# A two-layer decoder on one core: in the state space, four of sixteen input products per group made token-major by ScalarE and turned back by TensorE

## The reference, cut to what matters

```
xn = layernorm(x); x_in, z = split(xn @ W_in)            # 256 inner channels
u  = silu(causal_conv4(x_in) + b)
dt_r, B, C = split(u @ W_xproj)                          # 8, 16 and 16 columns
dt = softplus(dt_r @ W_dt + b_dt)
for n in 16 states:  h[n,t] = h[n,t-1]*exp(dt[t]*A[n]) + dt[t]*u[t]*B[t,n]
y  = sum_n h[n,t]*C[t,n] + u*D;  out = x + (y*silu(z)) @ W_out
```

## Time and profile before

| | us |
|---|---|
| median of 3 runs | 1837.51 (1835.39 to 1838.07) |
| the profiled execution, its own time | 1837.73 |
| its span in the profile | 1836.0 |
| PE busy | 1472.0 (80%) |
| DVE busy | 1420.9 (77%) |
| POOL busy | 895.3 (49%) |
| ACT busy | 877.3 (48%) |
| state space, 706.8 to 1199.7 us: length | 492.9 |
| DVE busy in it | 462.44 |
| PE busy in it | 388.08 |
| POOL busy in it | 384.75 |
| ACT busy in it | 290.10 |

### The profile page before, as it was taken

One profiled execution on the slowest core, in us unless ns is written; L12 is line 12 of the kernel. 1 busy time (PEld: TensorE's weight loads), 2 busy tenths in 40 slices (PEclk: granted clock), 3 DMA queues, 4 the chain that ended last, 5 costly groups with the idle time before them and its releaser, 6 DMA issues. The chain is left out here.

```text
span 1836.0 us, 29627 instructions
## 1 busy us (share of the span) xinstructions
PE 1472.0 (80%) x9959; PEld 988.1 (54%) x9963; DVE 1420.9 (77%) x2912; ACT 877.3 (48%) x1352; POOL 895.3 (49%) x790
## 2 busy tenths in 40 slices
...
DMA packets 86142, 142.86 MB, mean 78 GB/s; under 512 B 13098, under 2 KB 38866, under 8 KB 85506
## 3 DMA queue, kind: packets, MB, share of 16 engines
q1 hardware_dynamic: 80610, 131.63, 22.5%
...
## 5 line engine op out<-in xcount | busy, mean ns | idle before, releaser
L1564 POOL TENSOR_TENSOR m_hC<-m_h,m_Cs 128x1024 f32<-128x1024 f32 x128 | 300.8, 2355 | 109.3 <-PE PS L1813 64.4
L1813 PE MATMUL PS<-m_hC,identf 128*128 128x512 f32 x512 | 269.8, 657 | 91.1 <-POOL m_hC L1564 90.3
L1734 DVE TENSOR_TENSOR_SCAN m_h<-m_dA,PS 128x512 f32<-128x512 f32 x256 | 297.3, 1204 | 0.1
L1813 PEld LDWEIGHTS PS<-m_hC,identf 128*128 128x128 f32 x512 | 97.3, 203 | 243.6 <-POOL m_hC L1564 143.1
L1678 ACT ACTIVATE m_dA<-m_DT,m_A 128x508 f32<-128x508 f32 x256 | 169.5, 712 | 47.4 <-DVE m_h L1734 36.6
L1728 DVE TENSOR_TENSOR PS<-PS,m_Bs 128x512 f32<-128x512 f32 x256 | 163.0, 683 | 2.0 <-ACT PS L1669 2.0
L2267 PE MATMUL PS<-e_xT,e_WT 128*128 128x128 f32 x1136 | 140.6, 278 | 0.0
L2025 ACT ACTIVATE e_Sg<-PS 128x512 f32<-128x512 f32 x71 | 42.4, 597 | 198.2 <-PE PS L2267 198.2
...
L2267 PEld LDWEIGHTS PS<-e_xT,e_WT 128*128 128x128 f32 x1136 | 134.6, 194 | 0.0
L2182 DVE TENSOR_TENSOR e_HT<-PS,e_Sg 128x512 f32<-128x512 f32 x71 | 49.1, 692 | 101.8 <-PE PS L2267 101.8
L82 POOL TENSOR_TENSOR ln_lv<-ln_mv,ln_eps 128x4 f32<-128x4 f32 x24 | 4.8, 200 | 223.3 <-DVE ln_mv L75 223.3
...
...
## 6 DMA issues: line engine op xcount, KB each, us to landing
...
m_Bs<-state_rows SPq DMA_DIRECT2D x128, 256.0 KB, 3.2
m_Cs<-state_rows SPq DMA_DIRECT2D x128, 256.0 KB, 3.4
...
```

What stands on the lines that cost most here:

```text
L1564: nc.gpsimd.tensor_tensor(hC[:, G % NY], hst[:, G % NH], wide(Cs[:, G % RB, :]), ALU.mult).then_inc(s["hC"], 1)
L1734: nc.vector.tensor_tensor_scan(hst[:, G % NH, ch, :], dA[:, G % NA, ch].rearrange("p b l -> p (b l)"), bank(DBU + ch), 0.0, ALU.mult, ALU. ...
L1813: ins = nc.tensor.matmul(bank(YB + ch), c.identf[:, :], hC[:, G % NY, ch, :], start=False, stop=(n == NS - 1))
```

## The change

**State space.** In groups 1 to 7 the input products of states 9, 11, 13 and 15 leave DVE. ACT makes them with the tokens on the partitions, where B[t,n] is one number per partition: four scaled copies of 256 columns for each state (`scaled`, from `DUT` and `BT` into the buffer `E2`, which the softplus of the next group also uses, so that the first waits for `corrected0`). PE turns them back with eight transposes (`turn`). To have the operands token-major, PE turns dt*u (`tokens0`, `tokens1`) and B (`bt`), and ACT copies them (`tokens_copy0`, `tokens_copy1`, `bt_copy`). `m_hC` gets a third buffer. The row transfers of B for the turned states fall away. Many places in `OWN` move.

**Experts.** `te` is found ahead of `offs`; two multiplications and two sums become one each; the tables are made from 16-bit numbers in pairs; one small multiplication (`Cp`) of each Sinkhorn round moves to where DVE waits for PE.

```diff
-    NH, NY, NA, RB = 4, 2, 4, 4
+    NH, NY, NA, RB = 4, 3, 4, 4
...
-           "silus": -13.6, "dt_b_c": -15.5, "parts": -11.6, "dt0": -12.5, "dt1": -12.4, "dt_bias": -7.5, "exps": -6.5, "logs": -5.5,
-           "corrected0": -8.5, "corrected1": -7.5, "softplus": -6.5, "inputs": -5.5, "z0": -8.5, "z1": -7.5, "z_copy0": -3.4, "z_copy1": -2.4,
...
+           "silus": -13.6, "dt_b_c": -15.5, "parts": -11.6, "dt0": -13.5, "dt1": -13.4, "dt_bias": -9.6, "exps": -8.5, "logs": -7.5,
+           "corrected0": -10.5, "corrected1": -8.5, "softplus": -6.5, "inputs": -4.5, "z0": -8.5, "z1": -7.5, "z_copy0": -3.4, "z_copy1": -2.4,
+           "staged": 1.5, "gate": 17.5, "output0": 22.6, "output1": 23.6, "stats": 26.5, "rstd": 26.6, "norm": 30.5, "silu_z": 16.5,
+           "bt": -11.9, "bt_copy": -8.1, "tokens0": 4.5, "tokens1": 5.5, "tokens_copy0": 8.6, "tokens_copy1": 9.6}
...
+    TURNED = (9, 11, 13, 15)
+    turned = lambda G: G >= NS and G % NS in TURNED
...
+        if turn is not None:
+            due += [(G + ahead, turn, G // NS, G % NS) for G in range(NG * NS) if turned(G)]
...
+            def b_copied(g, par):
+                act.wait_ge(s["bt"], g)
...
+                nc.scalar.copy(BT[:, par].rearrange("p b n -> p (b n)"), PS[:, 0, 0:GB * NS]).then_inc(s["btc"], 1)
...
+            def scaled(g, n):
+
+                k = len(TURNED) * (g - 1) + TURNED.index(n)
+                act.wait_ge(s["tc"], CH * g)
+                act.wait_ge(s["btc"], g)
+                act.wait_ge(s["dBu"], CH * (g * NS + n - 1))
+                if n == TURNED[0] and g + 1 < NG:
+                    act.wait_ge(s["t"], 2 * g + 1)
+                for b in range(GB):
+                    ins = nc.scalar.activation(E2.rearrange("p c (b l) -> p (c b) l", b=GB)[:, CH * b:CH * b + CH, :], DUT[:, b], ACT.Copy, scale=BT[:, g % 2, b, n:n + 1])
+                ins.then_inc(s["sc"], 1)
...
-            run(lambda: None, step, stages)
+            run(lambda: None, step, stages, scaled, 1.55)
...
-                for ch in range(CH):
+                for ch in range(0 if turned(G) else CH):
...
+            def b_tokens(g, par):
+                pe.wait_ge(s["ab"], g * CH + CH)
+                for b in range(GB):
+                    ins = nc.tensor.transpose(PS[:, 0, b * NS:(b + 1) * NS], xd[0:NS, b * P:(b + 1) * P], c.identf[0:NS, 0:NS])
+                ins.then_inc(s["bt"], 1)
...
+            def turn(g, n):
+
+                G = g * NS + n
+                pe.wait_ge(s["sc"], len(TURNED) * (g - 1) + TURNED.index(n) + 1)
+                for ch in range(CH):
+                    pe.wait_ge(s["h"], CH * (G - 1) + ch + 1)
+                    for b in range(GB):
+                        ins = nc.tensor.transpose(PS[:, DBU + ch, b * P:(b + 1) * P], E2.rearrange("p c (b l) -> p (c b) l", b=GB)[:, CH * b + ch, :], c.identf[:, :])
+                    ins.then_inc(s["dBu"], 1)
...
-            run(setup, step, stages)
+            run(setup, step, stages, turn, -2.05)
...
+            step(nc.vector.tensor_tensor(both[:, :, :, :], both[:, :, :, :], pos[:, :, :].rearrange("p (o b) e -> p o b e", o=1).to_broadcast([P, 2, B, NE]), ALU.mult))
+            step(nc.vector.tensor_reduce(pk[:, :], both[:, :, :, :].rearrange("p k b e -> p (k b) e"), AX_X, ALU.add))
...
-                nc.vector.tensor_tensor(OS[:, m, :], along(iota[:, :], P), each(sq[:, m], P), ALU.is_equal).then_inc(s["os"], 1)
...
+                nc.vector.tensor_tensor(OS[:, h], number(P), along(sq[:, m], P), ALU.is_equal).then_inc(s["os"], 1)
```

More of the change, by code:

```diff
@@ L1439, in state_space @@
     OWN = {"inner_stats": -25.5, "inner_rstd": -25.4, "inner_norm": -20.5, "xn_T": -22.5, "xn_copy": -16.6, "x0": -20.5, "x1": -19.5, "x2": -18.5, "x3": -17.5,
-           "silus": -13.6, "dt_b_c": -15.5, "parts": -11.6, "dt0": -12.5, "dt1": -12.4, "dt_bias": -7.5, "exps": -6.5, "logs": -5.5,
-           "corrected0": -8.5, "corrected1": -7.5, "softplus": -6.5, "inputs": -5.5, "z0": -8.5, "z1": -7.5, "z_copy0": -3.4, "z_copy1": -2.4,
-           "staged": 1.5, "gate": 17.5, "output0": 21.6, "output1": 22.6, "stats": 25.5, "rstd": 25.6, "norm": 30.5, "silu_z": 16.5}
@@ L1445, in state_space @@
+           "bt": -11.9, "bt_copy": -8.1, "tokens0": 4.5, "tokens1": 5.5, "tokens_copy0": 8.6, "tokens_copy1": 9.6}
+    EARLY = {0: {"first_inputs": -1, "gate": 18.5, "z0": -1, "z1": 0.5, "z_copy0": 1.4, "z_copy1": 2.4,
+                 "output0": 23.6, "output1": 24.6, "stats": 26.5, "rstd": 26.6, "norm": 30.2},
              1: {"inner_stats": 0.5, "inner_rstd": 0.4, "inner_norm": 4.4, "xn_T": 1.5, "xn_copy": 6.4, "x0": 2.5, "x1": 2.6, "x2": 3.5, "x3": 4.5, "silus": 9.4,
                  "dt_b_c": 6.5, "parts": 11.4, "dt0": 7.5, "dt1": 7.6, "dt_bias": 13.1, "exps": 13.2, "logs": 13.3, "corrected0": 10.5, "corrected1": 10.6,
-                 "softplus": 11.5, "inputs": 11.6, "z0": 8.5, "z1": 9.5, "z_copy0": 14.4, "z_copy1": 15.4},
+                 "softplus": 11.5, "inputs": 11.6, "bt": 8.4, "bt_copy": 13.15, "z0": 8.5, "z1": 9.5, "z_copy0": 14.4, "z_copy1": 15.4},
@@ L1452, in state_space, with run @@
     LATE = 2
     STORE = [16] + [g * NS + 11 for g in range(1, NG - 1)]
-    LATER = ("corrected0", "corrected1", "softplus", "inputs", "staged")
+    LATER = ("corrected0", "corrected1", "softplus", "inputs", "staged", "bt", "bt_copy", "tokens0", "tokens1", "tokens_copy0", "tokens_copy1")
+    TURNED = (9, 11, 13, 15)
+    turned = lambda G: G >= NS and G % NS in TURNED
+    by_rows = [G for G in range(NG * NS) if not turned(G)]
     def aux(g, ch):
         return bank((1 if g == 0 else 7, 0)[ch])
-    def run(setup, step, stages):
+    def run(setup, step, stages, turn=None, ahead=0.0):
@@ L1486, in store @@
                 if g >= 2:
-                    for ready in bs + cr:
-                        sp.wait_ge(ready, 16 * (g - 1) * NS // RB)
+                    for i in range(RB):
+                        sp.wait_ge(bs[i], 16 * len([at for at, G in enumerate(by_rows) if at % RB == i and G < (g - 1) * NS]))
+                        sp.wait_ge(cr[i], 16 * (g - 1) * NS // RB)
                 sp.dma_start(c.BCD[g % 2], xd[0:32, :]).then_inc(s["bcs"], 16)
```

127 lines of the change are left out of this document (84 added, 43 removed).

## The result

The changed kernel took 1846.4 us (median of 5 runs, 1844.98 to 1850.04), the kernel before 1838.07 (5 runs beside them): ratio 1.0054, 95% interval 1.0042 to 1.0066. It is slower by half a per cent; the forecast was 1845. The profiled execution has a span of 1843.2 us.

The account below looks back on a forecast made before the run. DVE was taken as the bound (462 of 493 us), with only 3 us a group over POOL and PE. State space +10, PE's clock +7.5 and experts -10 gave +7.5 on 1837.5: 1845 us; 8 in 10 within 1820 to 1861.

Parts of the forecast that it names:

- signs of being wrong: Profile readings that would refute the forecast: gates less than 61 us apart, or DVE's waits at state 13 under 4 us.
- The new wait of POOL: State space, POOL: `corrected0` comes next after the product of state 5 and waits 3.5 us for ACT's `logs`.
- The chain to state 13: After the gate: `rstd` starts at 41.7 us, `norm` 43.4, copies done 46.6, scan of state 13 starts 47.2.
- DVE alone would be there at 38.9: DVE, without waiting for the turn, would reach the scan of state 13 38.9 us after the gate; scan forecast at 47.2.
- The turn of state 15: PE: behind step 11, `x0`, step 12 and `x1`, it ends at 54.3 us; DVE, there at 52.9, waits 1.4 us.
- The gate: State space, middle groups: the next gate comes 63.5 us behind the last, where it was 61.3.
- the clock's term: PE at half clock after waits: slow step 11 adds 1.5 us a group in groups 1 to 5, +7.5 (0 to 17).
- Groups: Gate to gate without clock: group 1 60.8 to 66.1, groups 2-5 249.0 to 254.0, 6 58.0 to 60.4, 7 54.9 to 51.5.
- The experts: Experts: tables -9.1, `te` and joined instructions +1.1, `Cp` -1, first gather -1; sum -10 us, from -12 to -1.
- Cp: Experts, Sinkhorn rounds on DVE: 14 of these multiplications leave the path, some 0.07 us each by the starts: -1 us.
- `corrected0` does not wait: Rival: POOL starts with the product of state 5, `rstd` at 38.2, a group takes 60 us; 1820 us. Chance 0.17.
- DVE keeps what it gains: Rival: copies for state 13 are in time, a group takes 53.7 to 56 us; 1783 to 1803 us. Chance 0.06.

Follow-up runs that it names:

- The two turns of state 13: Changed kernel with `corrected0` one product later (1828.57 us): this turn in two neighbouring groups, once at full clock, once at half; groups of 61.1 and 62.4 us.
- the part alone: Only the experts' part of the change put into the kernel before, state space as before: 1830.98 us, ratio 0.9952.
- everything moved: Changed kernel with `corrected0`, `norm`, turn of state 15, `Cp`, group 1's special places, then `softplus` and `inputs` moved: 1810.82 us, ratio 0.9859 to the kernel before.

## Why the prediction was right, and where its steps were not

The time was right (1845 forecast, 1846.4 measured; 7.5 us more forecast, 8.3 by the medians and 9.9 by the ratio), and so, within 2 us each, were its three terms (state space, clock, experts). The picture of the waits was partly wrong. One of the prediction's own signs of being wrong came true: it named DVE's waits at state 13 under 4 us, and they were 3.0; of the other signs, POOL's wait ahead of `corrected0`, gates without a wait and 63 to 66 us apart in the middle came out right, and the tables' round was 3.01 us instead of 2.9. That the total came within 2 us in spite of this is in part luck: the 4.9 us of waits that it did not see, at states 9 and 11, did not lengthen the chain that set the time, and two falls of the clock in a group cost together what one had been priced at.

- *What DVE saves*: 33 us forecast, 33.5 measured. *What the parts cost*: the four copies 1.8 us forecast and 1.70 measured, a turn 0.9 and 1.04.
- *The new wait of POOL*: 3.5 us ahead of `corrected0` forecast, 3.30 measured, `logs` ending 20.6 us behind the gate (20.9).
- *The chain to state 13*: `rstd` at 41.0 behind the gate (forecast 41.7), `norm` at 42.7 (43.4), the copies done at 45.8 (46.6), the scan at 47.0 (47.2). Each is within 0.9 us.
- *"DVE alone would be there at 38.9"*: it was there at 43.9. This step failed: the prediction followed POOL's delay only into `rstd`, not into PE's list, where step 6 and so the turn of state 9 stand behind the same late product. DVE had already waited 4.9 us at states 9 and 11, so it waited 3.0 at state 13, not 8.3. The sum hardly moved, since the scan's start was set by the later chain over `rstd` and `norm`, whatever DVE had waited before. That the place of `corrected0` is the cause is shown: moved by one product it gave 18 us back.
- *The turn of state 15*: 1.4 us forecast without the clock, 3.2 measured, the scan 1.6 us later than forecast.
- *The gate*: 63.5 forecast without the clock, 64.96 measured; 1.5 a group was the clock's term. Kept at full clock the group took 63.3 us and the kernel 7.8 us less: the size of the term of +7.5 is shown. Its place was only half right: the prediction saw one slow place, the clock fell at two (step 6 took 3.60 us instead of 1.88, too). The two turns of state 13 show 1.3 us for that place.
- *Groups* (forecast with 1.5 each for the clock in groups 1 to 5): group 1 67.6, measured 68.0; groups 2 to 5 260.0, measured 259.9; group 6 60.4 and 60.7; group 7 51.5 and 51.3. Sum of the distances: +16.8 forecast, +17.2 measured.
- *The first gate*, +0.9: not to be told, as the first gates of these kernels lie up to 6 us apart in no order that follows the edits.
- *The third buffer*: nothing, shown.
- *The experts*: -10 forecast; behind the last gate 624.8 us instead of 633.0, -8.2, and -8.8 by the part alone. In the profiles of all kernels with the new tables that stretch lies between 622.0 and 628.2 us, so its last 3 us can't be told from one profile. From the last product of E to the ids 28.9 us instead of 36.9, the -8.0 of the prediction (-9.1 and +1.1). The first gather was waited for some 1.2 us less (-1 forecast). *Cp* failed: forecast -1, measured +1.1. "14 of them leave the path" was wrong, since they had lain in 0.5 us in which DVE could not start the next sum anyway.
- *The rule of the Trainium skill* ("VectorE: DVE Perf Modes", "What auto-detection actually checks"): the trace agrees. `OS` with only 16-bit tensors took 1.22 us for 2048 columns, 2.29 with two 32-bit operands, although both operands are broadcast over a dimension outside the pairs.

Of the rivals, "`corrected0` does not wait" was the near one: made true by an edit in groups 2 to 6, it gave 1828.6 us rather than 1820. With groups 1 to 6 each 3 us shorter than in the prediction's sum the distances would add up to 414 us; they add up to 422.7. Of the 8.7 us 4.8 lie in group 1, which the edit left alone, and 3.7 in groups 2 to 5, 1.9 of them in the one whose turn of state 13 ran at the lower clock. The place of the turn of state 15 is not the reason: its move took groups 2 to 5 from 60.7 to 60.6 us. "DVE keeps what it gains" is the one that none of the kernels reached: with everything moved a group took 59.4 us, against 53.9 of DVE's work.
